# Moving twelve shared-expert products and three short steps at the entry of a state-space mixer (Trainium2, one core)

## The chip, the cores and the metric

The kernel runs on one core of one Trainium2 chip. The metric is the device time of one launch in microseconds (us): 862.42 us is the median of three runs (861.83 to 862.47). TensorE is PE in the rows, VectorE is DVE, ScalarE is ACT, GpSimd is POOL and SyncE is SP. Each of them executes its own list of instructions in order, and they wait for one another through semaphores.

## The reference, cut to what matters

Input x has 2 x 2048 tokens of 256 numbers.

```python
x = x + 0.5 * ffn(layernorm(x))      # layer 0: shared expert + one routed expert of 8 per token
x = x + mixer(layernorm(x))          # W_in, causal conv of 4 taps, 16-state recursion, silu, W_out
x = x + 0.5 * ffn(layernorm(x))      # layer 1: the same weights again

ffn:   shared = (silu(x @ sg.T) * (x @ su.T)) @ sd.T
       routed = sigmoid(max logit) * the same form with the chosen expert's weights
mixer: u = conv4(x @ W_in + b_in) + conv_b
       h = tanh(A) h + u Bp;  y = Cp . h + Dp u
       out = silu(y) @ W_out + b_out
```

The recursion is the same linear filter for every channel, so the kernel applies it to the normalized rows before W_in, as products with a Toeplitz matrix plus a small carried state.

## The kernel before, in words

The 4096 tokens are 8 groups of 512 (four tiles of 128 rows). Every float32 product is made of three products of a high and a low part, so each operand is rounded (`hi`, on ScalarE) and its remainder subtracted (`lo`, on VectorE or GpSimd).

Order of the whole: layer 0's normalization and routing, four groups through the shared expert, 39 routed slots, the other four groups through the shared expert, the mixer over the 8 groups, then layer 1's feed-forward in the same form. The order on each engine is written out by hand; nothing is planned at run time.

The change lies where layer 0's last shared group ends and the mixer begins, at about 365 to 400 us of the span.

- TensorE, `shared` (L547 on): for the last group of layer 0 the shared down products are mixed with the first chunks of the mixer. `shared_down(L, g, fb, tokens)` makes three products for each 128 rows, into banks `D2[0]` (first two tiles) and `D2[1]` (last two). The last twelve products (fb 2 and 3, tiles 2 and 3) stand behind `w_in_part(0, 0)` and `w_in_part(0, 1)`.
- TensorE, `attention` (L762 on), iteration n: `w_out_part(n-2, 1..3)`, `w_in_part(n, 0)` and `(n, 1)`, the transposes of a finished group, `b_out_part(n-1)`, `mix_chunk(n+1, 0)`, `w_out_part(n-1, 0)`, `w_in_part(n, 2)`, `mix_chunk(n+1, 1)`, `w_in_part(n, 3)`, logits. `w_in_part(n, cb)` alternates between two banks, so it waits until the taps of the block two before have been read out (`s_v`); it also waits for the low part of the mixed rows (`s_zl`, written by `mix_lo`). `mix_chunk(n+1, 0)` waits for `ln2_lo(n+1)` (`s_xnl`); its second half waits for `state_lo` (`s_hhl`). `b_out_part(0)` waits for the last shared sum (`s_add`).
- ScalarE, `attention` (L1074 on): `first_tap(n, cb)` scales a W_in bank into `v`, `y_silu` is the silu of `v`, `y_round` its high part (into `y_hi`, which is the buffer `hT_hi` of the shared expert), `mix_hi` the high part of the mixed rows (it waits until all of W_in of the group before has been computed), `ln2_apply` and `ln2_hi` the normalized rows.
- VectorE, `attention` (L1555 on): `taps(n, cb)` adds the other three taps (three instructions), then `mix_lo`, `state_lo`, `ln2_lo`, `ln2_stats` and `ln3_stats` (mean and variance of a group, four `bn_stats` and four `bn_aggr`), `add_out`, `add_shared`.
- GpSimd (the loop behind `ln2_rsqrt(2)` of its list), iteration n: `y_low(n-2, 3)`, `ln3_rsqrt(n-3)`, `y_low(n-1, 0)`, `add_bias(n-1, 2)`, `ln2_rsqrt(n+2)` if n > 0, `y_low(n-1, 1)`, `add_bias(n-1, 3)`, one or two gathers of group 3, for even n >= 2 `conv_bias`, `edge_bias(n)`, `y_low(n-1, 2)`, `add_bias(n, 0)`, `add_bias(n, 1)`. `ln2_rsqrt(k)` first waits for `ln2_stats(k)`. `add_bias(n, cb)` follows the taps, `y_silu(n, cb)` follows `add_bias`.

Of the kernel before, what the change touches and what calls it, by code (L numbers as in the profile page):

```python
# [30 lines left out]
def build(nc, x, w_routed, w_shared, gate_w, w_in, w_out, vecs, b_in, b_out, ssm_a, ssm_bc, ssm_d, out):  # L31
# [41 lines left out]
    with ExitStack() as ctx:  # L73
# [300 lines left out]
        def half_groups(L, half): return ORDER[L][1:NH + 1] if half == 0 else ORDER[L][NH + 1:]  # L374
# [45 lines left out]
        def live(n): return 0 <= n < NG  # L420
# [9 lines left out]
        def _(pe):  # L430
# [99 lines left out]
            def shared_down(L, g, fb, tokens=range(GT)):  # L530
                n = c_s(L, g)
                pe.wait_ge(s_hl, 4 * n + fb + 1)
                for t in tokens:
                    ts = slice(t * P, (t + 1) * P)
                    cs = slice(DN0 + fb * H, DN0 + (fb + 1) * H)
                    mm = mm3(pe, D2[t // 2][:, (t % 2) * H:(t % 2 + 1) * H], hT_hi[:, fb, ts],
                             hT_lo[:, fb, ts], ws_hi[:, cs], ws_lo[:, cs],
                             start=(fb == 0 and t % 2 == 0), stop=(fb == FB - 1))
                    if fb == FB - 1 and t % 2 == 1:
                        mm.then_inc(s_d, 1)  # L540

            def shared(L, half):

                groups = half_groups(L, half)
                for i, g in enumerate(groups):
                    first, last = i == 0, g == groups[-1]
                    shared_gu(L, g, 0)  # L547
                    if L == 0 and half == 0 and first:
                        prefix(L, PF[L])
                    shared_gu(L, g, 1)  # L550
                    if L == 0 and half == 0:
                        setup_part(i)
                    shared_gu(L, g, 2)
                    shared_gu(L, g, 3)
                    if L == 0 and half == 1 and last:
                        pe.wait_ge(s_ainit, 1)
                        shared_down(L, g, 0, range(2))
                        shared_down(L, g, 1, range(2))
                        pe.wait_ge(s_h, 4 * NG)
                        mix_chunk(0, 0, 0)  # L560
                        mix_chunk(0, 1, 0)
                    if half == 1 and first:
                        pe.wait_ge(s_ye, (L + 1) * NS)
                        if L == 0:
                            pe.wait_ge(s_wfix, KB)
                    if L == 0 and half == 1 and last:
                        shared_down(L, g, 2, range(2))
                        shared_down(L, g, 3, range(2))
                        shared_down(L, g, 0, range(2, 4))
                        shared_down(L, g, 1, range(2, 4))  # L570
                        pe.wait_ge(s_wiol, 2)
                        w_in_part(0, 0)
                        w_in_part(0, 1)
                        shared_down(L, g, 2, range(2, 4))
                        shared_down(L, g, 3, range(2, 4))
                    elif L == 1 and half == 1 and last:
                        for fb, a in ((0, 0), (1, 0), (2, 0), (0, 1), (3, 0), (1, 1), (2, 1), (3, 1)):
                            shared_down(L, g, fb, range(2 * a, 2 * a + 2))
                    else:
                        for fb in range(FB):  # L580
                            if half == 0 and last and fb == FB - 1:
                                m_transpose(L, 0, 0, 0)
                            shared_down(L, g, fb)
# [177 lines left out]
            def attention():  # L761
                for n in range(NG + 1):  # L762
                    if live(n - 2):
                        w_out_part(n - 2, 1)
                        w_out_part(n - 2, 2)
                        w_out_part(n - 2, 3)
                    if live(n) and n > 0:
                        w_in_part(n, 0)
                        w_in_part(n, 1)
                    if live(n - 3):  # L770
                        ln3_transposes(n - 3, 2 * min(n + 1, NG))
                    if live(n - 1):
                        b_out_part(n - 1)
                    if live(n + 1):
                        mix_chunk(n + 1, 0, max(n - 2, 0))
                    if live(n - 1):
                        w_out_part(n - 1, 0)
                    if live(n):
                        w_in_part(n, 2)
                    if live(n + 1):  # L780
                        mix_chunk(n + 1, 1, max(n - 2, 0))
                    if live(n):
                        w_in_part(n, 3)
                    if live(n - 3) and n < NG:
                        logits(f_ln3(n - 3))
# [96 lines left out]
        def _(act):  # L882
# [128 lines left out]
            def state_hi(n, c):  # L1011
                act.wait_ge(s_stp, 2 * n + c + 1)
                hi(HH[:, n % NB, :], SB_[:, 0:FH]).then_inc(s_hhh, 1)
# [40 lines left out]

            def y_round(n, cb):
                act.wait_ge(s_y, 4 * n + cb + 1)
                if n > 0:
                    if cb < CB - 1:
                        act.wait_ge(s_oc, 3 * (n - 1) + cb + 1)
                    else:  # L1060
                        act.wait_ge(s_o, 2 * n)
                hi(y_hi[:, cb, :], v[:, n % 2, cb, :]).then_inc(s_yh, 1)

            def attention():
                ln2_apply(1)
                state_hi(0, 0)
                state_hi(0, 1)
                mix_hi(0)
                ln2_hi(1)
                for n in range(NG):  # L1070
                    if live(n - 1):
                        y_silu(n - 1, 2)
                    if live(n):
                        first_tap(n, 0)  # L1074
                        first_tap(n, 1)
                    if live(n - 1):
                        y_round(n - 1, 2)
                    if live(n - 3):
                        ln3_copy(n - 3)
                    if live(n - 1):  # L1080
                        y_silu(n - 1, 3)
                    if live(n + 1):
                        state_hi(n + 1, 0)
                    if live(n + 2):
                        ln2_apply(n + 2)
                    if live(n - 1):
                        y_round(n - 1, 3)
                    if live(n):
                        y_silu(n, 0)
                        first_tap(n, 2)  # L1090
                        y_round(n, 0)
                    if live(n + 1):
                        mix_hi(n + 1)
                    if live(n):
                        y_silu(n, 1)
                        first_tap(n, 3)
                        y_round(n, 1)
                    if live(n + 1):
                        state_hi(n + 1, 1)
                    if live(n - 2):  # L1100
                        ln3_apply(n - 2)
                    if live(n + 2):
                        ln2_hi(n + 2)
# [103 lines left out]
        def _(dve):  # L1207
# [347 lines left out]
            def attention():  # L1555
                ln2_lo(1)
                for n in range(NG):
                    if live(n) and n > 0:
                        state_lo(n, 0)
                    if live(n - 3):  # L1560
                        ln3_stats(n - 3)
                    if live(n + 2) and n > 0:
                        ln2_stats(n + 2)
                    if live(n - 1):
                        taps(n - 1, 2)
                    if live(n) and n > 0:
                        mix_lo(n)
                    if live(n - 4):
                        copy_logits(group_of(n - 4), f_ln3(n - 4) + 1)
                    if live(n - 1):  # L1570
                        taps(n - 1, 3)
                    if live(n - 2):
                        add_out(n - 2, 0)
                        add_out(n - 2, 1)
                    if live(n) and n > 0:
                        state_lo(n, 1)
                    if live(n + 1) and n > 0:
                        ln2_lo(n + 1)
                    if live(n):
                        taps(n, 0)  # L1580
                        taps(n, 1)
                    if n == 0:
                        add_shared(0, half_groups(0, 1)[-1], (1,))

            def attention_end():
                g, n = ORDER[1][0], NG - 1
# [608 lines left out]
```

## Time and profile before

| | |
|---|---|
| median of three runs | 862.42 us |
| the profiled execution | 862.49 us, its span 860.6 us |
| TensorE busy | 828.5 us, 96% of the span |
| VectorE, ScalarE, GpSimd busy | 484.4, 391.5, 463.1 us |
| mean granted TensorE clock | 0.99 of full |

The span runs from the first to the last instruction that the profiler recorded. A busy share over the whole span is a mean of stages with different limits, so the argument is made from the timelines of the engines between 365 and 465 us. In a row of a timeline the first number is the start, the second the time, and the brackets give the idle time before it and who ended it.

### The profile page before, as it was taken

The page shows a single profiled execution, that of the slowest core. Times are in us where ns is not written, and L with a number is a line of the kernel's source. Part 1 is how long each engine was busy: PE and PEld are TensorE (multiplying, and loading weights), DVE is VectorE, ACT ScalarE, POOL GpSimd, SP SyncE. Part 2 cuts the span into 40 slices and gives each one's busy share as a digit, 9 for nine tenths or more (in the row PEclk, how much of TensorE's full clock was granted, in tenths as well). Part 3 has the DMA queues.
Part 4 walks back from the last instruction along what each step waited for, and adds up shares of the span by engine and source line. Part 5 has one row for each costly group of instructions (what it writes and reads, how often), then busy time and mean ns, then how long its engine had stood idle before and what let it go on. Part 6 is the DMA issues. An engine that isn't in the chain of part 4 may idle for free.

```text
span 860.6 us, 16215 instructions
## 1 busy us (share of the span) xinstructions
PE 828.5 (96%) x5302; PEld 721.7 (84%) x5303; DVE 484.4 (56%) x981; ACT 391.5 (45%) x766; POOL 463.1 (54%) x444
## 2 busy tenths in 40 slices
PE   4999999999999999999999999999999999999995
PEld 3778988888888888888888888888888888888884
DVE  7788753333333336678999986767333333333454
ACT  4743323334334334556777786233244334343331
POOL 6528870333334058859999982687331243330684
PEclk9999999999999999998999999999999999999998
DMA  9973553646565337310010015255345555421565
GB/s 310 324 260 105 177 166 118 208 165 203 168 212 173 102 67 141 44 26 13 7 57 26 26 51 196 66 162 188 124 139 185 205 197 195 156 101 43 117 153 159
DMA packets 52389, 119.07 MB, mean 138 GB/s; under 512 B 6442, under 2 KB 40372, under 8 KB 47988
## 3 DMA queue, kind: packets, MB, share of 16 engines
q0 software_dynamic: 17008, 75.25, 27.9%
q1 hardware_dynamic: 34834, 43.15, 15.5%
q8 instruction: 31, 0.51, 0.2%
q14 instruction: 18, 0.15, 0.1%
q10 hardware_dynamic: 498, 0.02, 0.0%
HBM read 83.25 MB, written 35.14 MB: 138 GB/s over the span
## 4 chain that ended last, share of the span: by engine, by line
PE 72%; POOL 12%; DVE 7%; issue 3%; DMA 3%; ACT 1%; POOLq 0%; DVEq 0%; SPq 0%
PE bank L424 21%; PE bank L426 20%; PE bank L425 20%; POOL xs_sorted L1858 4%; PE bank L631 4%; DVE v L1544 3%; POOL yr L2052 3%; POOL acc L1932 2%; DMA wr_hi<-w_routed 2%; PE bank L600 2%; POOL wr_lo L1902 2%; PE bank L491 1%; PE bank L502 1%; POOL wr_lo L1894 1%; DVE stats L1226 1%
## 5 line engine op out<-in xcount | busy, mean ns | idle before, releaser
L1902 POOL TENSOR_TENSOR wr_lo<-wr_raw,wr_hi 128x3072 fp32r<-128x3072 f32 x14 | 95.4, 6818 | 96.0 <-DMA wr_hi<-w_routed 87.7
L424 PE MATMUL bank<-wr_hi,xT_hi 128*128 x312 | 130.2, 417 | 1.2 <-POOL wr_lo L1902 1.2
L1209 DVE TENSOR_TENSOR hT_lo<-bank,hT_hi 128x512 fp32r<-128x512 f32 x78 | 54.0, 692 | 124.6 <-ACT hT_hi L884 124.6
L1502 DVE TENSOR_TENSOR hf<-sg,bank 128x512 f32<-128x512 f32 x78 | 53.7, 688 | 124.3 <-PE bank L426 124.3
L426 PE MATMUL bank<-wr_lo,xT_hi 128*128 x312 | 123.4, 396 | 0.0
L425 PE MATMUL bank<-wr_hi,xT_lo 128*128 x312 | 122.9, 394 | 0.0
L1932 POOL DMA_INDIRECT acc<-ys_sorted,pos x44 | 70.8, 1609 | 79.3 <-issue 49.3
L424 PE MATMUL bank<-xT_hi,ws_hi 128*128 128x512 f32 x256 | 102.4, 400 | 2.2 <-DVE xT_lo L1209 2.2
L425 PE MATMUL bank<-xT_hi,ws_lo 128*128 128x512 f32 x256 | 100.8, 394 | 0.0
L426 PE MATMUL bank<-xT_lo,ws_hi 128*128 128x512 f32 x256 | 100.7, 393 | 0.0
L911 ACT ACTIVATE sg<-bank 128x512 f32<-128x512 f32 x64 | 38.3, 598 | 126.4 <-PE bank L426 126.3
L424 PE MATMUL bank<-wr_hi,hT_hi 128*128 x312 | 93.9, 301 | 1.5 <-DVE hT_lo L1209 1.5
L426 PE MATMUL bank<-wr_lo,hT_hi 128*128 x312 | 87.3, 280 | 0.0
L425 PE MATMUL bank<-wr_hi,hT_lo 128*128 x312 | 87.2, 279 | 0.0
L884 ACT ACTIVATE xT_hi<-bank 128x256 fp32r<-128x256 f32 (+1 forms) x102 | 43.2, 435 | 92.8 <-PE bank L600 84.7
L1312 DVE TENSOR_TENSOR hf<-sg,bank 128x512 f32<-128x512 f32 x64 | 43.6, 683 | 63.0 <-PE bank L426 59.8
L974 ACT ACTIVATE sg<-bank 128x512 f32<-128x512 f32 x78 | 46.6, 597 | 68.0 <-PE bank L426 68.0
L1544 DVE SCALAR_TENSOR_TENSOR v<-bank,vec,v 128x511 f32<-128x511 f32 (+2 forms) x96 | 71.0, 746 | 8.7 <-ACT v L1048 6.0
L424 PE MATMUL bank<-ws_hi,hT_hi 128*128 128x256 f32 x256 | 73.5, 287 | 0.1
L425 PE MATMUL bank<-ws_hi,hT_lo 128*128 128x256 f32 x256 | 72.4, 283 | 0.0
L426 PE MATMUL bank<-ws_lo,hT_hi 128*128 128x256 f32 x256 | 72.4, 283 | 0.0
L1876 POOL DMA_DIRECT2D wr_hi<-w_routed x16 | 9.0, 562 | 115.1 <-PE bank L426 115.1
(248 smaller groups left out, 2180.7 us busy)
## 6 DMA issues: line engine op xcount, KB each, us to landing
wr_raw<-w_routed POOLq DMA_DIRECT2D x16, 1536.0 KB, 7.2
wr_hi<-w_routed POOLq DMA_DIRECT2D x16, 1536.0 KB, 7.8
rows<-xs_sorted SPq DMA_DIRECT2D x78, 128.0 KB, 2.4
ys_sorted<-rows SPq DMA_DIRECT2D x78, 128.0 KB, 1.7
xg<-xT_kept SPq DMA_DIRECT2D x12, 512.0 KB, 4.2
xT_kept<-xTf SPq DMA_DIRECT2D x9, 512.0 KB, 3.2
acc<-x SPq DMA_DIRECT2D x8, 512.0 KB, 9.8
xs_sorted<-zeros POOLq DMA_DIRECT2D x4, 1024.0 KB, 8.3
```

The lines of the kernel that those rows point to most:

```text
L424: pe.matmul(o, a_hi, b_hi, start=start, stop=False, skip_group_check=True)
L425: pe.matmul(o, a_lo, b_hi, start=False, stop=False, skip_group_check=True)
L426: return pe.matmul(o, a_hi, b_lo, start=False, stop=stop, skip_group_check=True)
L884: return act.activation(o, i, ACT.Copy)
L911: act.activation(sg[:, fb % 2, :], G2[fb % 2][:, :], ACT.Silu).then_inc(s_sg, 1)
L974: act.activation(sg[:, 0, :], MG[:, :], ACT.Silu).then_inc(s_msg, 1)
L1209: return dve.tensor_tensor(o, full, f32(h), ALU.subtract)
L1312: dve.tensor_tensor(hf[:, fb % 2, :], sg[:, fb % 2, :], U2[fb % 2][:, :], ALU.mult).then_inc(s_h, 1)
L1502: dve.tensor_tensor(hf[:, 0, :], sg[:, 0, :], MU[:, :], ALU.mult).then_inc(s_mh, 1)
L1544: dve.scalar_tensor_tensor(vb_[:, d:GN], UB[cb % 2][:, 0:GN - d], vec[:, cb, k:k + 1], vb_[:, d:GN], ALU.mult, ALU.add).then_inc(s_tap if ...
L1902: pool.tensor_tensor(wr_lo[:, e % 2, :], wr_raw[:, :], f32(wr_hi[:, e % 2, :]), ALU.subtract).then_inc(s_wl, 1)
L1932: pool.indirect_dma_start(out=acc[:, tt, :], out_offset=None, in_=ys_dram, in_offset=bass.IndirectOffsetOnAxis(ap=pos[:, tt:tt + 1], axis= ...
```

## The change

TensorE: the last twelve shared down products leave their place behind `w_in_part(0, 1)` and stand in iteration n = 1 of the mixer, ahead of `w_in_part(1, 0)`. ScalarE: `first_tap(0, 2)` stands ahead of `ln2_apply(2)`, `y_silu(0, 0)` and `y_round(0, 0)`; `y_round(0, 2)` and `(0, 3)` get a wait for the end of the shared down products, as they write a buffer that those read. VectorE: the last shared sum, `add_shared(0, ..., (1,))`, and `ln2_stats(3)` stand behind `taps(0, 3)` instead of ahead of `state_lo(1, 0)` and `taps(0, 2)`. Every computed value stays the same.

```diff
@@ TensorE, shared
                         w_in_part(0, 0)
                         w_in_part(0, 1)
-                        shared_down(L, g, 2, range(2, 4))
-                        shared_down(L, g, 3, range(2, 4))
@@ TensorE, attention
+                    if n == 1:
+                        g = half_groups(0, 1)[-1]
+                        shared_down(0, g, 2, range(2, 4))
+                        shared_down(0, g, 3, range(2, 4))
                     if live(n) and n > 0:
                         w_in_part(n, 0)
                         w_in_part(n, 1)
@@ ScalarE
             def y_round(n, cb):
                 act.wait_ge(s_y, 4 * n + cb + 1)
+                if n == 0 and cb >= 2:
+                    act.wait_ge(s_d, 2 * NG)
...
+                    if n == 0:
+                        first_tap(n, 2)
                     if live(n + 2):
                         ln2_apply(n + 2)
...
                         y_silu(n, 0)
-                        first_tap(n, 2)
+                        if n > 0:
+                            first_tap(n, 2)
@@ VectorE
-                    if live(n + 2) and n > 0:
+                    if live(n + 2) and n > 1:
                         ln2_stats(n + 2)
...
                         taps(n - 1, 3)
+                    if n == 1:
+                        add_shared(0, half_groups(0, 1)[-1], (1,))
+                        ln2_stats(n + 2)
...
                         taps(n, 1)
-                    if n == 0:
-                        add_shared(0, half_groups(0, 1)[-1], (1,))
```

## Rows read from the trace of the kernel before

**Rows 1.** Windows: busy time of PE, PEld, DVE, ACT, POOL; clock; DMA share, GB/s.

```profile
388.90:395.70 6.80, 6.02 (x23) 5.06 (x21) 6.57 (x9) 3.38 (x8) 6.16 (x7) 0.50 0.01 1
...
396.00:407.00 11.00, 11.00 (x84) 10.45 (x84) 7.53 (x17) 8.11 (x18) 10.32 (x12) 1.00 0.15 22
402.00:501.00 99.00, 97.63 (x727) 87.60 (x727) 91.08 (x175) 74.78 (x155) 93.53 (x136) 1.00 0.08 25
```

**Rows 2.** Chain that ended last, from 403 to 447 us, by line.

```profile
by line: DVE v L1544 42.2%; DVE xl L1209 12.4%; DVE stats L1226 12.3%; DVE acc L1552 8.1%; issue 6.7%; DVE xT_lo L1209 5.4%; DVE HH L1209 4.8%; DVE mv L1230 3.4%; ACT xT_hi L884 2.5%; ACT v L1048 1.3%; ACT v L1053 0.8%; PE bank L426 0.6%; P
```

**Rows 3.** Timeline of TensorE.

```profile
376.50 0.28 PE L424 MATMUL bank<-ws_hi,hT_hi 128*128 128x256 f32 x1
...
377.92 0.28 PE L424 MATMUL bank<-tt_hi,xh 128*128 128x256 f32 x1
...
380.13 0.40 PE L424 MATMUL bank<-xT_hi,win_hi 128*128 128x512 f32 x1
...
384.91 0.40 PE L426 MATMUL bank<-xT_lo,win_hi 128*128 128x512 f32 x1
387.51 0.50 PE L424 MATMUL bank<-xT_hi,win_hi 128*128 128x512 f32 x1 [2.20 <-DVE xT_lo L1209]
...
390.09 0.77 PE L424 MATMUL bank<-xT_hi,win_hi 128*128 128x512 f32 x1 [0.78 <-DVE v L1544]
...
463.16 0.47 PE L424 MATMUL bank<-xT_hi,win_hi 128*128 128x512 f32 x1
```

**Rows 4.** Timeline of VectorE.

```profile
376.08 4.54 DVE L1544 SCALAR_TENSOR_TENSOR v<-bank,vec,v 128x511 f32<-128x511 f32 x6 [1.12 <-ACT v L1048]
380.54 0.68 DVE L1361 SCALAR_TENSOR_TENSOR acc<-bank,acc 128x512 f32<-128x512 f32 x1
...
381.71 1.40 DVE L1226 BATCH_NORM_STATS2 stats<-acc 128x6 f32<-128x256 f32 x4
383.26 0.64 DVE L1230 BATCH_NORM_AGGREGATE mv<-stats 128x2 f32<-128x6 f32 x4 [0.15 <-DVE stats L1226]
...
386.17 1.28 DVE L1209 TENSOR_TENSOR xT_lo<-bank,xT_hi 128x512 fp32r<-128x512 f32 x2
387.62 2.32 DVE L1544 SCALAR_TENSOR_TENSOR v<-bank,vec,v 128x511 f32<-128x511 f32 x3 [0.17 <-ACT v L1048]
...
390.43 1.53 DVE L1209 TENSOR_TENSOR xl<-xg,xh 128x1024 fp32r<-128x1024 f32 x1
...
401.07 2.32 DVE L1544 SCALAR_TENSOR_TENSOR v<-bank,vec,v 128x511 f32<-128x511 f32 x3 [1.26 <-ACT v L1048]
...
457.08 2.32 DVE L1544 SCALAR_TENSOR_TENSOR v<-bank,vec,v 128x511 f32<-128x511 f32 x3 [0.43 <-ACT v L1048]
```

**Rows 5.** Timeline of ScalarE.

```profile
380.61 2.07 ACT L1001 ACTIVATE xg<-acc,shift,rstd 128x256 f32<-128x256 f32 x4
...
385.35 1.08 ACT L884 ACTIVATE xT_hi<-bank 128x512 fp32r<-128x512 f32 x2 [1.00 <-PE bank L426]
...
399.78 0.62 ACT L1053 ACTIVATE v<-v 128x512 f32<-128x512 f32 x1
...
400.35 0.68 ACT L1048 ACTIVATE v<-bank,vec 128x512 f32<-128x512 f32 x1
...
455.78 0.63 ACT L1053 ACTIVATE v<-v 128x512 f32<-128x512 f32 x1 [2.50 <-POOL v L1830]
```

**Rows 6.** Timeline of GpSimd.

```profile
387.70 0.24 POOL L1747 TENSOR_SCALAR ve<-mv 128x4 f32<-128x4 f32 x1
...
389.60 1.27 POOL L1834 TENSOR_TENSOR hT_lo<-v,hT_hi 128x512 fp32r<-128x512 f32 x1
390.83 2.27 POOL L1830 TENSOR_TENSOR v<-v,cbs 128x512 f32<-128x512 f32 x1
...
395.23 1.57 POOL L1932 DMA_INDIRECT acc<-ys_sorted,pos  x1 [0.30 <-issue]
...
397.48 3.12 POOL L1830 TENSOR_TENSOR v<-v,cbs 128x512 f32<-128x512 f32 x2
```

## The prediction, made before the changed kernel was run

> **What bounds the kernel now.** I read the busy shares first: TensorE is busy nearly always, so the question is where it stops, and what starts it again. The windows by clock come next. From 388.9 to 395.7 us the granted clock is 0.50, which is 1.2 GHz, and it is full in the stretches behind [rows 1]. The timeline of TensorE shows why that stretch is special: W_in of group 0 ends with the product of 384.91, the next one starts only at 387.51 behind `mix_lo(1)`, and after six products there is a second stop, until 390.09, behind `taps(0, 3)` [rows 3]. Products of this size follow each other every 0.23 us, so the stops cost 387.51 - 385.14 = 2.4 us and about 1.1 us. During the half clock the next six products and the four of `b_out` run at half rate.
>
> But the chain from 403 to 447 us does not lie on TensorE: over nine tenths of it are VectorE's lines [rows 2]. VectorE waited for ScalarE before the taps at 401.07 (1.26 us) [rows 4] and from 402 to 501 us it is busy for 91.1 of 99 us, GpSimd for 93.5 and TensorE for 97.6 [rows 1]. Three engines run with almost no slack, so time saved on TensorE before 400 us reaches the end only if VectorE and GpSimd are early too. At 457.08 VectorE waits 0.43 us for a first tap, which stands behind a silu that waited 2.50 us for GpSimd's `add_bias` [rows 4, 5]. And TensorE's product of 463.16 starts 0.1 us behind the taps that follow. So GpSimd's time reaches TensorE there.
>
> **The change part by part.** I write the new times in the profile's clock; nothing before 376.50 changes.
>
> *TensorE.* The twelve products took 377.92 - 376.50 = 1.42 us, a mixing chunk 380.13 - 377.92 = 2.21 us; from 380.13 to the end of the product of 384.91 (385.14) lie two blocks of W_in and one chunk, so a block is (5.01 - 2.21) / 2 = 1.40 us [rows 3]. New: chunk 376.50 to 378.71, block (0,2) to 380.11, chunk to 382.32, block (0,3) to 383.72, the twelve products to 385.14. No work is added or removed.
>
> *ScalarE.* A step that waits for a block starts 0.2 us behind it (385.35 after 385.14 [rows 3, 5]), so `first_tap(0, 2)` starts at 380.3; its two instructions take 0.75 us (400.35 + 0.68 less their start beside the silu of 399.78 [rows 5]), to 381.1. `ln2_apply(2)` (2.07), `y_silu(0, 0)` and `y_round(0, 0)` follow and end at 384.2 [rows 5]; only then comes `mix_hi(1)`, 384.1 instead of 385.35. It no longer waits for TensorE (ready at 383.9), but for its own queue. The new wait of `y_round(0, 2)` is for products that end at 385.1, and it comes at about 391: nothing.
>
> *VectorE.* The first taps end at 380.62 [rows 4], `state_lo(1, 0)` at 381.1, `taps(0, 2)` run from 381.1 to 383.4. The sum (0.68) and the statistics (381.71 to 383.90, about 2.1) are gone from ahead of it, but it now idles 1.35 us until `mix_lo(1)` at 384.8 to 386.05. TensorE's block (1,0) starts at 386.1 instead of 387.51: its first stop shrinks from 2.4 to 1.0 us. `taps(0, 3)` follow ScalarE at 386.4 to 388.7 (before 387.62 to 389.94), block (1,1) starts at 388.85 instead of 390.09. So far 1.25 us are gained.
>
> Now the moved steps: the sum 388.65 to 389.3, statistics to about 391.2, `state_lo(1, 1)` to 391.65. `ln2_lo(2)` starts there, not at 390.43 [rows 4]. TensorE has finished block (1,1) and `b_out` at 390.7 at full clock, or 392.3 at half, and waits for it until about 393 (or 393.9, below), where before it reached this chunk at 393.64: the gain is gone on TensorE.
>
> *GpSimd.* This decides. `ln2_rsqrt(3)` keeps its place ahead of `y_low(0, 1)`, `add_bias(0, 3)`, two gathers, `y_low(0, 2)` and `add_bias(1, 0)`, and it waits for the statistics. Before, they were ready at 383.9 and the step ran without a wait from 387.70 to 389.60 [rows 6]. Now GpSimd is free at 387.0 and stands until 391.25: step to 393.2, or 3.6 us later. Beside this is a cost that I bound from both sides. The `add_bias` of 390.83 took 2.27 us and the `y_low` before it 1.27 [rows 6]; in that time VectorE's `ln2_lo` of 390.43 ran 1.53 us [rows 4]: the two seem to exclude each other, which cost GpSimd 1.0 us. In the new order `ln2_lo(2)` (from 391.65) falls into the rsqrt steps, and `add_bias(0, 3)` escapes. So the 1.0 us is either saved (delay 2.6 us) or paid at the other place (3.7 us), and then `ln2_lo(2)` itself may be 0.95 us late. I take the nearer to the second, as VectorE's instruction is one block against four short ones.
>
> The Trainium skill (SBUF - State Buffer, "SBUF: two separate sides") says that VectorE and GpSimd share a port pair as an exclusive lock, held for a whole instruction. The 2.27 against 1.27 us agrees, and by that rule the upper end would hold.
>
> GpSimd's second gather ended at 395.23 + 1.57 = 396.8, `y_low(0, 2)` and the two `add_bias` at 400.6 [rows 6], that is 1.27 each, so `add_bias(1, 0)` ended at about 399.35; `y_silu(1, 0)` started at 399.78 [rows 5], which is 0.4 us of slack. The delay at this silu is thus 2.6 - 0.4 = 2.2 us to 3.7 - 0.4 = 3.3 us. `first_tap(1, 2)` and the taps of 401.07 stand behind it and move to 403.3 to 404.4 [rows 4, 5]. `mix_lo(2)` and `taps(1, 3)` win back some of it, as before they had small waits, but GpSimd's `add_bias(1, 2)` follows the taps, and from there GpSimd has no gap to catch up in [rows 1]. Each later silu of block 0 carries its delay to VectorE, at 457.08 without slack [rows 5, 4], and from there with the loss of at most 0.1 us to TensorE's block at 463.16 [rows 3]. TensorE does the rest of the kernel later by that.
>
> Sum: +2.2 to +3.3 us, of which I take +2.7 on the profiled execution's 862.49 us, 865.2. It lies 0.07 above the median, so the forecast is 865.1 us, 0.3% slower. What the half clock does is worth little here: with it TensorE's block (1,3) ends at about 403.8, before ScalarE takes up `mix_hi(2)` at 404.3 or later.
>
> **The rivals.**
>
> *A. The delay is won back in part.* GpSimd's spans are rough and its rows hide small waits; and a contact of `ln2_lo` with an `add_bias` costs 1.0 us each time. If the shift lets GpSimd escape one or two of the contacts between 402 and 447 us, the end is 2.7 - 1.0 or 2.7 - 2.0 = +0.7 to +1.7, or 863.7 us. For it: VectorE, not GpSimd, is the chain there [rows 2]. Against it: both engines move by nearly the same time, so the contacts stay.
>
> *B. Faster.* The place is VectorE from 396 to 407 us: it is busy for 7.5 of 11 us there [rows 1], and its waits, among them the 1.26 us of 401.07 [rows 4], come from TensorE's half clock. If most of these 3.5 us vanish, less the 1.7 us of new idle time that I found before 386.4 (1.35 before `mix_lo(1)`, 0.35 before `taps(0, 3)`), the end is some 1.5 us earlier: 860.9 us. It decides if GpSimd's `add_bias(1, 0)` ends before 399.7; for that the rsqrt of group 3 would have to start within 0.4 us of its old time, and the statistics are computed 7 us later than before.
>
> *C. Slower still.* TensorE's new stop ahead of `mix_chunk(2, 0)` is as long as the one of 2.20 us. If the clock stays at half for a second stretch of 6.8 us [rows 1], 3.4 us of TensorE's time are lost, of which the late ScalarE covers about 2.4: +1.0 more, 866.1 us.
>
> The Trainium skill (TensorE: Matmul & The Clock Gate, "What you observe" and what follows) says that idleness halves TensorE's clock and activity restores it. The trace agrees: full up to the stops, 0.50 behind them. If the earlier block kept the clock full, the rule would speak for B, which needs GpSimd all the same.
>
> **How the numbers follow.** Forecast 0.55, A 0.25, B 0.12, C 0.08. The range leaves out most of B and the end of C: 862.0 to 866.4 us. A measurement of this kernel can tell 0.2% (1.7 us) from no change, so "slower" begins at 864.1: nearly all of the forecast's case (0.50), C (0.08) and a small part of A (0.05) give 0.63; the rest of the forecast and of A, and a little of B, give 0.26; B gives 0.11.
>
> **What the profile after would show.** Right: TensorE's first stop is about 1.0 us and starts again at 386.1; GpSimd idles some 4 us before the rsqrt of group 3, with VectorE's statistics as the releaser; TensorE waits for `xl` before the chunk of group 2; the taps of 401.07 start at 403.3 to 404.4; the product of 463.16 comes 2 to 3 us later. I am wrong if GpSimd's wait is there but the block of 463.16 is not late (A), or if VectorE's taps of block (1,2) are not later than 401 us (B).

## The result and the profile after

The changed kernel takes 865.93 us (865.33 to 866.59, six runs) against 862.20 for the kernel before (861.03 to 863.25, six runs): ratio 1.0043, 95% interval 1.0029 to 1.0057. It is slower by 3.7 us, 0.4%. The forecast was 865.1 us, within 862.0 to 866.4. The profiled execution took 866.08 us with a span of 864.2.

In this execution the stage begins 0.4 us earlier than in the one of before (the first taps start at 375.68, before at 376.08 [rows 4]); that is added wherever a delay is given below as "against the same start". It differs from execution to execution: in the twelve profiled here, the first taps start between 374.86 and 376.43.

The windows of the changed kernel, in the columns of [rows 1]:

```profile
388.90:395.70 6.80, 4.85 (x37) 4.42 (x36) 6.45 (x15) 1.27 (x3) 4.53 (x6) 1.00 0.00 0
...
402.00:501.00 99.00, 93.26 (x697) 82.80 (x696) 88.12 (x172) 73.75 (x156) 94.41 (x131) 1.00 0.08 25
```

The half clock of [rows 1] is gone (1.00 in place of 0.50), and yet TensorE is busy for only 93.3 of the 99 us behind 402 where it was 97.6. In these 99 us GpSimd alone has no more idle time than before (94.4 us busy, before 93.5). Its timeline shows where it lost time ahead of them:

```profile
390.92 0.24 POOL L1755 TENSOR_SCALAR ve<-mv 128x4 f32<-128x4 f32 x1 [4.51 <-DVE mv L1237]
391.24 2.10 POOL L1758 TENSOR_TENSOR rstd<-ve,mhalf 128x4 f32<-128x4 f32 x1
...
393.88 1.29 POOL L1842 TENSOR_TENSOR hT_lo<-v,hT_hi 128x512 fp32r<-128x512 f32 x1
...
400.79 3.12 POOL L1838 TENSOR_TENSOR v<-v,cbs 128x512 f32<-128x512 f32 x2
```

It stands 4.51 us for the statistics of group 3, and its next `y_low` starts at 393.88 where it started at 389.60 [rows 6]. The pair of `add_bias` behind the gathers starts at 400.79, before at 397.48: 3.7 us late against the same start. ScalarE and VectorE behind it:

```profile
402.72 0.63 ACT L1055 ACTIVATE v<-v 128x512 f32<-128x512 f32 x1 [2.87 <-POOL v L1838]
...
459.33 0.63 ACT L1055 ACTIVATE v<-v 128x512 f32<-128x512 f32 x1 [3.33 <-POOL v L1838]
```

```profile
384.32 1.29 DVE L1216 TENSOR_TENSOR xT_lo<-bank,xT_hi 128x512 fp32r<-128x512 f32 x2 [1.30 <-ACT xT_hi L886]
...
391.21 1.23 DVE L1216 TENSOR_TENSOR xl<-xg,xh 128x1024 fp32r<-128x1024 f32 x1
...
404.02 2.32 DVE L1551 SCALAR_TENSOR_TENSOR v<-bank,vec,v 128x511 f32<-128x511 f32 x3 [4.24 <-ACT v L1050]
```

The silu of block (1,0) waits 2.87 us for GpSimd and VectorE's taps of (1,2) 4.24 us for the first tap; in [rows 4] this wait was 1.26. TensorE feels it last:

```profile
385.67 0.50 PE L424 MATMUL bank<-xT_hi,win_hi 128*128 128x512 f32 x1 [0.75 <-DVE xT_lo L1216]
...
392.49 0.39 PE L424 MATMUL bank<-tt_hi,xh 128*128 128x256 f32 x1 [1.95 <-DVE xl L1216]
...
466.71 0.47 PE L424 MATMUL bank<-xT_hi,win_hi 128*128 128x512 f32 x1 [0.84 <-DVE v L1551]
```

The first stop shrinks from 2.20 us [rows 3] to 0.75, as intended, and the same product that ran at 463.16 (block 1 of group 5) now runs at 466.71: 3.55 us later, 3.95 against the same start. The chain from 403 to 447 us has changed hands:

```profile
by line: DVE v L1551 20.2%; POOL v L1838 11.5%; POOL hT_lo L1842 8.6%; PE bank L424 6.6%; PE bank L426 6.4%; PE bank L425 6.3%; POOL cbs L1800 6.2%; issue 6.2%; POOL acc L1940 5.6%; DVE xT_lo L1216 5.4%; ACT v L1050 2.7%; POOL rstd L1758 2.
```

In [rows 2] no line of GpSimd was among the first ones; now its lines shown make up about a third.

### The profile page after: what moved, and what is told of

Read it like the earlier page. It is cut to its first block, busy times and chain, and to the rows that moved or that the text cites. A ratio compares the mean times of both kernels' runs of the same rounds, so it can differ in the third digit from the quotient of the medians.

```text
span 864.2 us, 16217 instructions
## 1 busy us (share of the span) xinstructions
PE 825.7 (96%) x5302; PEld 718.5 (83%) x5303; DVE 481.9 (56%) x981; ACT 390.8 (45%) x766; POOL 463.3 (54%) x444
## 4 chain that ended last, share of the span: by engine, by line
PE 69%; POOL 15%; DMA 5%; DVE 5%; issue 4%; ACT 1%; POOLq 0%; DVEq 0%; ACTq 0%; SPq 0%
PE bank L424 20%; PE bank L426 20%; PE bank L425 20%; POOL xs_sorted L1866 4%; PE bank L629 4%; POOL acc L1940 3%; POOL yr L2060 2%; DVE v L1551 2%; DMA wr_hi<-w_routed 2%; PE bank L598 2%; DMA xT_kept<-xTf_odd 2%; POOL wr_lo L1910 2%; PE bank L491 1%; POOL v L1838 1%; POOL wr_lo L1902 1%
```

## The experiments

Every kernel was timed in five rounds against the kernel before on the same chip (862.2 to 862.3 us in all three series). The changed kernel itself was timed in a measurement of its own, against 862.20 us. First, which part costs.

**Statistics back in their old place.** Edit against the changed kernel (VectorE):

```diff
-                    if live(n + 2) and n > 1:
+                    if live(n + 2) and n > 0:
                         ln2_stats(n + 2)
...
                         add_shared(0, half_groups(0, 1)[-1], (1,))
-                        ln2_stats(n + 2)
```

> The changed kernel with ln2_stats(3) back ahead of taps(0,2); products, first tap and the shared sum stay moved. Theory Q (GpSimd's queue is held by the late statistics, all the rest of the change is good): GpSimd's rsqrt of group 3 starts near 386.5 without a wait, the taps of block (1,2) start near 399.5 in place of 404.0, and the time is about 860.2 us, 2 us under the kernel before. Rival P (moving the products and the first tap costs, through the order on ScalarE and TensorE): it stays near 866 us. Rival S (both share it): 863 to 864 us.

Measured: 861.48 us, ratio 0.9989 (0.9980 to 0.9998). The other moves together are a small gain, barely clear of no change, and the whole loss hangs on this one. In its profiled execution the clock stayed full in the window of 388.9 to 395.7 us and GpSimd did not wait for the statistics. The gain is 0.8 us, not the 2 us expected; where the rest goes is the question of the second series.

**The kernel before with the statistics alone moved.**

```diff
-                    if live(n + 2) and n > 0:
+                    if live(n + 2) and n > 1:
                         ln2_stats(n + 2)
...
                         taps(n - 1, 3)
+                    if n == 1:
+                        ln2_stats(n + 2)
```

> The kernel before with one edit: ln2_stats(3) stands behind taps(0,3). Theory Q: the statistics end at about 391.7, half a us later than in the changed kernel, since taps(0,3) are later without the other moves; GpSimd stands some 4.5 us; the time is about 866.6 us, 4.4 over the kernel before. Rival P: the statistics alone cost little, 862 to 863 us.

Measured: 866.55 us, ratio 1.0043 (1.0029 to 1.0056); GpSimd's wait is 4.45 us. The one edit makes the whole loss by itself.

**Late statistics, but nothing queued behind the wait.** Edit against the changed kernel (GpSimd):

```diff
-                if live(n + 2) and n > 0:
+                if live(n + 2) and n > 1:
                     ln2_rsqrt(n + 2)
...
                     gather_tile(3, t, s_ga[3])
+                if n == 1:
+                    ln2_rsqrt(n + 2)
```

> The changed kernel, all its moves kept, but GpSimd takes the rsqrt of group 3 behind the two gathers instead of ahead of y_low(0,1). The statistics are as late as in the changed kernel; only what is queued behind the wait differs. Theory Q: y_low(0,1), add_bias(0,3) and the gathers no longer wait; the taps of block (1,2) start near 399.4; the time is about 860.3 us. Rival V (VectorE's order costs: the sum and statistics ahead of ln2_lo(2), which stops TensorE for 1.95 us): the stop stays and the time stays at 864 us or more.

Measured: 861.41 us, ratio 0.9989 (0.9980 to 0.9998) (860.3 us expected). GpSimd's rsqrt starts at 393.93 without a wait. TensorE's stop ahead of the chunk of group 2 is still there (1.96 us), so rival V falls. The lateness of the statistics costs nothing; what costs is the place at which GpSimd waits for them.

**How many instructions stand behind the wait.** The same edit with only `y_low(0, 1)` ahead of the rsqrt, and with `y_low(0, 1)` and `add_bias(0, 3)`:

```diff
                 if live(n - 1):
                     y_low(n - 1, 1)
+                    if n == 1:
+                        ln2_rsqrt(n + 2)
                     add_bias(n - 1, 3)
```

> The changed kernel with one instruction of GpSimd's queue, y_low(0,1), ahead of the rsqrt of group 3. If the loss is what is queued behind the waiting step (theory Q), it shrinks by that instruction's 1.27 us: about 864.7 us, against 865.9 of the changed kernel. If the loss has another root that the rsqrt itself carries (its result late for ln2_apply(3)), the time stays near 865.9 us.

> The same with two instructions ahead, y_low(0,1) and add_bias(0,3); the two gathers stay behind. Theory Q: 2.5 us less than the changed kernel, about 863.4 us (all four ahead gave 861.4). The other root: 865.9 us.

Measured: 864.78 us (ratio 1.0028, 1.0016 to 1.0040) and 863.61 us (1.0015, 1.0006 to 1.0025). With none ahead it was 865.93, with all four 861.41. The steps are 1.15, 1.17 and, for the two gathers together, 2.2 us. The interval of each of these times is about 1 us wide to either side, so the medians show the trend but not each step. The traces do. GpSimd with one instruction ahead:

```profile
390.12 0.24 POOL L1755 TENSOR_SCALAR ve<-mv 128x4 f32<-128x4 f32 x1 [3.10 <-DVE mv L1237]
```

| ahead of the wait | GpSimd's wait, us | first taps start | block 1 of group 5 starts | against the kernel before, same start |
|---|---|---|---|---|
| nothing (changed kernel) | 4.51 | 375.68 | 466.71 | +3.95 |
| `y_low(0, 1)` | 3.10 | 374.86 | 464.74 | +2.80 |
| and `add_bias(0, 3)` | 1.27 | 375.36 | 463.97 | +1.53 |
| and both gathers | none | 375.67 | 462.49 | -0.26 |

The first taps of the kernel before start at 376.08 and its block at 463.16. In the last two kernels GpSimd also waits 0.55 us for `taps(0, 3)`, ahead of `add_bias(0, 3)`. The first two instructions give back 1.15 and 1.27 us at that block; they take 1.29 and 1.30 us. The two gathers, which take 1.54 and 2.21 us here, give back only 1.8: no more than 1.27 us of waiting was left. So the price of the place is the wait itself, and an instruction moved ahead of it gives back its own time only until the wait is used up.

**`ln2_lo(2)` ahead of the statistics.** Edit against the changed kernel (VectorE):

```diff
                         add_shared(0, half_groups(0, 1)[-1], (1,))
-                        ln2_stats(n + 2)
...
                         ln2_lo(n + 1)
+                    if n == 1:
+                        ln2_stats(n + 2)
```

> The changed kernel, but on VectorE state_lo(1,1) and ln2_lo(2) stand ahead of ln2_stats(3), so TensorE's stop of 1.95 us before the chunk of group 2 shrinks to about 0.4, while the statistics end 1.7 us later. GpSimd's rsqrt then no longer meets ln2_lo(2) (its second step took 2.10 us in the changed kernel against 1.04 elsewhere). Theory Q: GpSimd's delay grows by 1.7 - 1.05 = 0.65 us, and the time to about 866.6 us. Rival V (TensorE's stop is what costs): about 864.3 us.

Measured: 867.05 us, ratio 1.0061 (1.0048 to 1.0075). TensorE's stop of 1.95 us went (no wait over 0.11 us there), GpSimd's rsqrt came later, and the kernel became slower: GpSimd decides, not the stop. Its timeline also shows the price of a meeting, as I call it when an instruction of GpSimd is held up by VectorE's `ln2_lo`:

```profile
392.56 0.24 POOL L1756 TENSOR_SCALAR ve<-mv 128x4 f32<-128x4 f32 x1 [6.23 <-DVE mv L1237]
392.88 1.05 POOL L1759 TENSOR_TENSOR rstd<-ve,mhalf 128x4 f32<-128x4 f32 x1
```

The power takes 1.05 us here, with VectorE in its taps (from 392.39), and 2.10 in the changed kernel, where VectorE's `ln2_lo` of 391.21 ran into it.

Second, where the rest of the gain goes. In the changed kernel and in the first and third experiment GpSimd needs 51.6 us from `add_bias(1, 2)` to `add_bias(4, 0)` (in the first experiment 454.26 - 402.67), with hardly a gap. So GpSimd's list was made shorter there.

**The gathers of group 3 spread otherwise.** They were two in n = 1 and one each in n = 2 and 3. Now two stand ahead of the loop, where GpSimd idled 3.69 us, and two in n = 1.

```diff
-            LAST_ROWS = {1: (0, 1), 2: (2,), 3: (3,)}
+            LAST_ROWS = {1: (2, 3)}
...
+            pool.wait_ge(s_add, 2 * NG - 1)
+            gather_tile(3, 0, s_ga[3])
+            gather_tile(3, 1, s_ga[3])
             for n in range(NG + 4):
...
-                    if n == 1 and t == 0:
+                    if n == 1 and t == 2:
                         pool.wait_ge(s_add, 2 * NG)
```

It was tried on the kernel with the rsqrt behind the gathers, on the kernel before, and on the one with the statistics back.

> The kernel e3_rsqrt_later with less GpSimd work behind 402 us: the first two gathers of group 3 stand ahead of the loop (they need only the first half of the last shared sum; GpSimd idled 3.7 us there), the last two in n = 1, none in n = 2 and 3. Theory Q2 (behind 402 us GpSimd's packed list, 51.6 us from add_bias(1,2) to add_bias(4,0), sets the pace and eats what is gained before it): that stretch shortens to about 49, TensorE's waits of 0.66, 0.50 and 0.85 us at block 1 of groups 3 to 5 vanish, and the time is about 859.3 us. Rival D (VectorE sets the pace there): those waits stay, and the time stays near 861.4.

> The kernel before with the same edit of the gathers and nothing else. In the kernel before VectorE was the chain from 403 to 447 us, so both theories expect little: Q2 861.7 us, rival D 862.2 us. A large gain, 860.5 us or less, would say that GpSimd bounded the kernel before as well.

> The kernel e1_stats_back with the same edit of the gathers. Theory Q2: as e5_rsqrt_later_gathers, about 859.5 us. Rival D: near 861.4 us.

Measured: 859.50 us (ratio 0.9979, 0.9969 to 0.9989), 859.63 us (0.9978, 0.9963 to 0.9992) and 859.34 us (0.9962, 0.9948 to 0.9976). GpSimd in the first of the three:

```profile
401.70 1.31 POOL L1838 TENSOR_TENSOR v<-v,cbs 128x512 f32<-128x512 f32 x1
...
450.05 2.53 POOL L1838 TENSOR_TENSOR v<-v,cbs 128x512 f32<-128x512 f32 x2
```

The stretch takes 48.4 us, and its windows read:

```profile
402.00:501.00 99.00, 98.30 (x735) 88.69 (x734) 92.06 (x177) 76.61 (x159) 92.01 (x135) 1.00 0.06 25
```

TensorE is busy for 98.3 of 99 us, and its waits at block 1 of groups 4 and 5 are gone, that of group 3 is down to 0.19 us: theory Q2 holds there. The miss is the second kernel: the kernel before gained 2.6 us from this edit, where at most 0.5 was expected. GpSimd bounded it as well, although the chain of [rows 2] named VectorE: two engines as close as these in [rows 1] can both hold the pace. The waits show it: between 395 and 475 us the silus of the kernel before waited 9.3 us for GpSimd in seven waits, with the gathers moved 4.4 us in four, and in neither did an engine wait for a DMA, so the gain is not that of rows that came sooner. Nor is it the clock's. In that kernel's profiled execution the mean in the window of 388.9 to 395.7 us was 0.86, not 0.50, but over the whole span its six timed runs had mean clocks of 0.990 to 0.995, and the 22 of the kernel before beside it 0.988 to 0.997. Of those 22, the five at 0.990 or less took 861.8 us in the median, the 13 at 0.994 or more 862.2: less clock did not make them slower. The three times do not differ by more than their intervals, so the last kernel is the best measured, but nothing shows that the changed kernel's other edits add to the gathers' gain.

**The sooner first tap taken back** (against the kernel with the statistics back):

```diff
-                    if n == 0:
-                        first_tap(n, 2)
                     if live(n + 2):
                         ln2_apply(n + 2)
...
-                        if n > 0:
-                            first_tap(n, 2)
+                        first_tap(n, 2)
```

> The kernel e1_stats_back with first_tap(0,2) back behind y_silu(0,0) on ScalarE: what is left of the change is the products and the shared sum. The statistics of group 3 stand ahead of those taps and end near 383.3, the first tap near 383.8, so it costs at most 0.4 us there: 861.5 us, no difference that can be measured. Rival F (the sooner first tap is where the gain of e1 comes from): 862.2 us or more.

Measured: 861.14 us, ratio 0.9985 (0.9976 to 0.9994), not to be told from 861.48. What gain that kernel has comes with the products and the shared sum, which were not tried apart; the first tap adds nothing that can be measured.

## Why the prediction was right

- **TensorE and VectorE up to 390 us.** `mix_lo(1)` was forecast at 384.8 and came at 384.32, 384.7 against the same start; the stop of TensorE at 1.0 us was 0.75 (0.9 counted as the forecast counts, from the spacing of the products: 384.64 + 0.12 to 385.67), the next start at 386.1 was 386.1 against the same start.
- **GpSimd's wait.** Forecast: from 387.0 to 391.25. The rows show 4.51 us, until 390.92 (391.3 against the same start). Experiments two and three show that this wait, with instructions queued behind it that do not need it, is the cause, and the table shows its price.
- **The meeting.** I bounded it by 1.0 us saved and 1.0 us paid. My argument spoke for the second, and yet the sum took +2.7, the middle of 2.2 and 3.3. It was paid in full: 2.10 against 1.05 us. The delay at the silu of (1,0) is 402.72 - 399.78 + 0.4 = 3.34 us, the upper end (3.3), and with 3.3 the forecast would have been 865.7.
- **The carry to TensorE.** I let it arrive with a loss of 0.1 us, and expected the product of 463.16 2 to 3 us later. It grew by 0.6 instead, to 3.95 (3.55 in the rows as they stand), so this sign failed on the high side. The term that I missed is in GpSimd's list:

```profile
406.42 1.27 POOL L1838 TENSOR_TENSOR v<-v,cbs 128x512 f32<-128x512 f32 x1
...
412.37 2.44 POOL L1940 DMA_INDIRECT acc<-ys_sorted,pos  x1 [0.17 <-issue]
...
458.01 1.29 POOL L1838 TENSOR_TENSOR v<-v,cbs 128x512 f32<-128x512 f32 x1
```

VectorE's `ln2_lo(3)` beside that gather, and the four rows of before that answer to these:

```profile
411.43 1.84 DVE L1216 TENSOR_TENSOR xl<-xg,xh 128x1024 fp32r<-128x1024 f32 x1
```

```profile
403.46 1.29 POOL L1830 TENSOR_TENSOR v<-v,cbs 128x512 f32<-128x512 f32 x1 [0.34 <-DVE v L1544]
...
409.57 1.66 POOL L1932 DMA_INDIRECT acc<-ys_sorted,pos  x1 [0.16 <-issue]
...
454.44 2.55 POOL L1830 TENSOR_TENSOR v<-v,cbs 128x512 f32<-128x512 f32 x2
```

```profile
409.70 1.22 DVE L1209 TENSOR_TENSOR xl<-xg,xh 128x1024 fp32r<-128x1024 f32 x1
```

In the new phase the gather of n = 2 starts while VectorE's `ln2_lo(3)` runs and takes 2.44 us, not 1.66; before, it was under way when `ln2_lo(3)` started. From `add_bias(1, 2)` to `add_bias(4, 0)` the list takes 458.01 - 406.42 = 51.6 us, before 454.44 - 403.46 = 51.0. So the mis-sized terms are this and the half of the meeting, and both made the loss larger: 3.7 us in place of 2.7.
- **The rivals.** A needed GpSimd to escape meetings; it had one more. B needed the silu not to be late. C needed a long half clock, and the clock stayed full in the profiled execution; its 1.0 us played no part. Of the six runs, the two with the lowest mean clock (0.994 and 0.995) took 865.33 and 865.78 us, no longer than the others. That a full clock did not help is what the forecast said of it. The first experiment has what B asked for, a full clock and no wait of GpSimd, and gained 0.8 us, not 1.5.

In the rows as they stand the block of group 5 is 3.55 us late and the span ends 3.6 us late, so nothing is regained behind it. The loss of 3.7 us lies 1 us above the forecast's 2.7, by the two terms above. Even the upper end of my sum (+3.3, or 865.7 us) is below the measured 865.93; the range holds it because it had room for C, which did not come about. The mechanism was right, and that its number stayed in the range was in part luck. What stays open: why the other moves of the change are worth about 1 us and not the 2 that were expected of them. GpSimd's list explains a part, as 0.6 us of it is the longer stretch of 51.6 us.

## What to carry to other kernels

When a producer is moved later, look not at who needs its result but at where in the consumer's queue the wait stands, and what is queued behind it without needing it. The whole wait is lost there, even where the result itself is needed much later; each instruction taken ahead of the wait gives back its own time until the wait is used up. A chain of waits that names one engine does not clear another one that is also packed; shortening the list of the packed one is the test. Moving the wait behind the work that does not need it was worth 4.5 us; all the other moves of the change together brought about 1.

## What the runs showed of the hardware

- VectorE's `ln2_lo` (two operands in SBUF, 128x1024) and GpSimd hold each other up: GpSimd's power took 2.10 us beside it and 1.05 without, and a gather that GpSimd issues took 2.44 us beside it and 1.66 without. A step of 0.20 us that started in the changed kernel at 430.39, just after the start of the `ln2_lo` of 430.30 to 431.52, took 1.19 us, to 431.58: it waited for the end of the whole instruction. It goes the other way too: the `ln2_lo` of 411.43, which started during an `add_bias`, took 1.84 us, not 1.22. The gather I had not expected. The Trainium skill (SBUF - State Buffer, "SBUF: two separate sides") has the lock, for a VectorE instruction with two SBUF inputs against one of GpSimd that reads SBUF, and the rows agree. It says that GpSimd is also kept from writing a transfer's descriptors, but of a VectorE copy in a two-port mode; the rows show a gather's issue lengthened by a subtraction.
- TensorE's clock was halved behind a stop of 2.1 to 2.2 us in three profiled kernels (before, the statistics alone, the gathers on the kernel before). It stayed at half for 6.8 us before, and for about 3.4 us (387.3 to 390.7) in the kernel with the gathers alone. Behind stops of 0.75, 1.10 and 1.95 us within 8 us it stayed full in the changed kernel, and behind the same stops (to 0.02 us) also in those with all four instructions ahead, with two, and with all four and the gathers moved. But in the kernel with one instruction ahead, behind stops of 0.76, 1.10 and 1.97 us, it fell to half from about 393.2 to 396.7 us. So the same stops left it full four times and halved it once, and it can't be counted on either way.
